# Self-attention in a decoder layer: the step's part of a projection is issued before the value matmuls, in the middle of the step

## The reference, cut to what matters

```python
qkv = x @ qkv_w + qkv_b
q, k, v = jnp.moveaxis(qkv.reshape(b, n, 3, H, D), 2, 0)
attn = jnp.einsum('bnhd,bmhd->bhnm', q, k) * scale
attn = jax.nn.softmax(attn, axis=-1)
out = jnp.einsum('bhnm,bmhd->bnhd', attn, v).reshape(b, n, c)
out = out @ proj_w + proj_b
```

## Time and profile before

| | |
|---|---|
| median of three runs | 4296.68 us |
| the profiled execution, its own time | 4303.63 us |
| its span, first to last instruction | 4302.0 us |
| TensorE busy over the span | 3724.0 us (87%) |
| granted TensorE clock, mean over the span | 0.932 |
| loop of self-attention | 202 to 2338 us of the span |

### The profile page before, as it was taken

One profiled execution on the slowest core, in us unless ns is written; L12 is line 12 of the kernel. 1 busy time (PEld: TensorE's weight loads), 2 busy tenths in 40 slices (PEclk: granted clock), 3 DMA queues, 4 the chain that ended last, 5 costly groups with the idle time before them and its releaser, 6 DMA issues. The chain is left out here.

```text
span 4302.0 us, 65605 instructions
## 1 busy us (share of the span) xinstructions
PE 3724.0 (87%) x17994; PEld 2267.9 (53%) x17995; DVE 2588.7 (60%) x4369; ACT 1651.5 (38%) x2902; POOL 2121.8 (49%) x1051
## 2 busy tenths in 40 slices
PE   4899999999999999999997688888549799887970
PEld 2445444454454544445454345445348688777860
DVE  3677776777767777677776454555324554444556
ACT  0055555555555555555554111111113343333430
POOL 0088888888888888888887112112220000000004
PEclk9799999999999999999998898898769899999985
DMA  5231211312113122131222201001022323233235
GB/s 190 82 88 44 80 54 50 93 39 80 56 48 94 38 80 58 47 94 38 80 57 70 75 30 59 29 29 59 10 78 95 120 79 108 89 106 101 98 101 171
DMA packets 202124, 322.52 MB, mean 75 GB/s; under 512 B 26107, under 2 KB 75675, under 8 KB 201797
## 3 DMA queue, kind: packets, MB, share of 16 engines
q1 hardware_dynamic: 182181, 266.45, 19.8%
q0 software_dynamic: 11168, 35.20, 2.6%
q10 hardware_dynamic: 8448, 16.78, 1.0%
HBM read 216.31 MB, written 46.44 MB: 61 GB/s over the span
## 5 line engine op out<-in xcount | busy, mean ns | idle before, releaser
L464 DVE TENSOR_REDUCE sa_part_max<-sa_mx 128x1 f32<-128x512 f32 x2124 | 1353.1, 681 | 575.7 <-PE sa_mx L579 573.5
L428 ACT ACTIVATE sa_prob<-sa_sc 128x512 f32<-128x512 f32 x2048 | 1117.9, 595 | 908.7 <-PE sa_sc L670 855.6
L268 POOL TENSOR_TENSOR sa_quad_sum<-sa_quad_sum,sa_prob 128x1024 f32<-128x1024 f32 x512 | 1205.3, 2393 | 0.0
L579 PE MATMUL sa_mx<-sa_k_stack,sa_q_stack 96*128 96x512 f32 x2124 | 1033.1, 491 | 23.2 <-issue 11.8
L670 PE MATMUL sa_sc<-sa_q_stack,sa_k_stack 98*128 98x512 f32 x2048 | 827.3, 404 | 7.4 <-ACT sa_prob L428 1.4
L268 POOL TENSOR_TENSOR sa_quad_sum<-sa_prob 128x1024 f32<-128x1024 f32 x256 | 617.3, 2433 | 406.0 <-ACT sa_prob L428 405.2
L579 PEld LDWEIGHTS sa_mx<-sa_k_stack,sa_q_stack 96*128 96x128 f32 x2124 | 407.6, 192 | 603.3 <-DVE sa_part_max L464 413.2
L1512 PE MATMUL ex_h<-ex_xT,ex_w 128*128 128x384 f32 (+2 forms) x2688 | 476.8, 334 | 117.0 <-issue 68.0
L593 PE MATMUL sa_pv<-sa_prob,sa_v 128*32 128x512 f32 x4104 | 552.1, 610 | 0.8 <-ACT sa_prob L428 0.8
L1512 PEld LDWEIGHTS ex_h<-ex_xT,ex_w 128*128 128x128 f32 x2688 | 457.8, 199 | 144.0 <-issue 121.7
L670 PEld LDWEIGHTS sa_sc<-sa_q_stack,sa_k_stack 98*128 98x128 f32 x2048 | 391.0, 191 | 176.1 <-ACT sa_prob L428 76.3
(11 more groups left out here) (178 smaller groups left out, 3397.9 us busy)
## 6 DMA issues: line engine op xcount, KB each, us to landing
sa_xT<-xT SPq DMA_DIRECT2D x70, 1024.0 KB, 5.2
ex_w_in<-in_L_ffn_w_dram SPq DMA_DIRECT2D x130, 512.0 KB
sa_k_stack<-sa_hilo SPq DMA_DIRECT2D x432, 64.0 KB, 2.0
sa_q_stack<-sa_hilo SPq DMA_DIRECT2D x408, 64.0 KB, 2.0
eo<-ex_out POOLq DMA_DIRECT2D x8, 1536.0 KB, 7.6
ca_aT<-attnT SPq DMA_DIRECT2D x9, 1024.0 KB, 7.1
ca_xb<-in_x_dram SPq DMA_DIRECT2D x9, 1024.0 KB, 9.0
attnT<-sa_recip SPq DMA_DIRECT2D x33, 256.0 KB, 2.4
```

The lines of the kernel that those rows point to most:

```text
L268: pool.tensor_tensor(quad_sum[:, i % 2, heads, :], so_far, prob[:, k, heads, :], ALU.add).then_inc(quad_ready, 1)
L428: act.activation(prob[:, kt % 4, j, :], sc[n % 2][:, :], ACT.Exp, scale=SCALE).then_inc(prob_ready, 1)
L464: dve.reduce_max(part_max[:, q, j, k:k + 1], mxp[bank % 3][:, :], AX_X).then_inc(max_read, 1)
L579: pe.matmul(mxp[bank % 3][:, :], q_stack[0:QK, j, at:at + P], k_stack[0:QK, buf, j, k * BANK:(k + 1) * BANK], start=True, stop=True).then_ ...
```

## The change

In each step that has a part of a projection, the call moves from behind head 3 to behind the score of head 1, ahead of `burst`. The instructions, their waits and their count stay the same; on the other engines nothing is edited.

```diff
                                 score(c, kt, i)
                                 if i == 1:
+                                    if (c, kt) in PART_AT:
+                                        project_part(*PART_AT[c, kt])
                                     burst(c, kt)
                                 if i == 2 and kt == T - EARLY:
                                     transpose_shift(at(NQ) + c + 1)
-                            if (c, kt) in PART_AT:
-                                project_part(*PART_AT[c, kt])
```

## The result

| | before | after |
|---|---|---|
| median | 4295.64 us (4 runs) | 4688.37 us (4678.99 to 4692.64, 4 runs) |
| span of the profiled execution | 4302.0 us | 4690.3 us |
| ratio to before | | 1.0911, 95% interval 1.0892 to 1.0931 |

The change makes the kernel 393 us, 9.1%, slower. The forecast was 4654 us, in a range of 4565 to 4745.

A forecast was written before the change was run, and what follows sets the result against it. The prediction took TensorE, in its written order, to bound the loop. Waits for `misc` (148 us), waits for exponentials (131) and clock falls (78) sum to 357 us, giving 4654 us, range 4565 to 4745.

The forecast's parts named there:

- term A: At kt 4 and kt 8, 64 first parts hold TensorE waiting for VectorE to release `misc`; 148 us.
- term B: At the end of all 384 steps with a part, scores wait for ScalarE's exponentials, 0.34 us each; 131 us.
- term C: Behind 60 of the 64 `misc` waits TensorE's granted clock falls to half, 1.3 us each; 78 us.
- The edits priced at nothing: Input DMAs, sequencing pauses at kt 0 and the 0.09 us passage from part to value matmuls: no added cost.
- (1): Rival: TensorE's clock holds through the single 2 to 3 us waits; 4576 us, chance 0.15.
- (2): Rival: the clock stays low longer, as in the 6.83 us stretch, another 78 us; 4732 us, chance 0.12.
- (3): Rival: exponentials don't bind at the step's end, as the longer middle lets ScalarE get ahead; 4523 us, chance 0.05.
- (4): Rival: `misc` is free in time, so no waits for it and no clock falls; 4428 us, chance 0.03.
- (5): Rival: faster, value weights load while the part streams, 35 us gained; 4262 us, chance 0.02.

The follow-up runs named there:

- e3: Changed kernel with 8 or 11 extra matmuls filling each of the 64 waits for `misc`; 4565.6 us, ratio 1.0632.
- e4: Changed kernel with VectorE taking the finished projection out of `misc` one step earlier; 4421.5 us, ratio 1.0295.
- e1: Changed kernel with the 64 first parts at kt 4 and kt 8 back at the step's end, 320 parts staying in the middle; 4415.0 us, ratio 1.0279.
- e5: Exponentials over 128 of 512 columns, attention not the reference's: on e4 4287.7 us (ratio 0.9988), on the kernel before 4268.8 us (0.9942).
- e2: Changed kernel with only the 64 first parts at kt 4 and kt 8 in the middle, the other 320 at the end; 4501.2 us, ratio 1.0481.
- e6: Kernel before, with VectorE emptying `misc` behind head 0's reading instead of head 1's and the four reciprocals one place earlier; 4264.1 us, ratio 0.9935.
- e10: e2 with its 64 waits filled by 8 matmuls (5 at kt 4 of chunk 3); 4438.1 us, ratio 1.0329.
- e8: e6 with the row sums of kt 14 moved from behind the value matmuls to the step's end; 4265.2 us, ratio 0.9932.

## Why the prediction was right, point by point

**The waits for `misc`, term A, 148 us: right, in place and length.** From the starts of scores in e3, at full clock, against before, less the 0.36 of term B, step by step: kt 4 of three chunks 7.55 - 4.57 - 0.36 = 2.62 us, kt 8 6.78 - 4.40 - 0.36 = 2.02, kt 4 of chunk 3 6.53 - 3.92 - 0.36 = 2.25. By 24, 32 and 8 this is 146 us. The 0.51 us that VectorE was to be later at kt 4 came out to the hundredth: 3.41 us behind the score, 2.90 before. e4 shows that the release, and not the matmuls behind it, is the cause.

**The exponentials, term B, 131 us: right.** 0.36 a step, 138 us over 384, of which 0.24 and 0.10 are the two waits of the earlier trace rows and the rest a few hundredths in the middle. e1 has it nearly alone (110 us for 320 steps), e5 removes it by its cause. So by the steps A and B make 284 us, where the sum had 279; at the starts of units 7 us go back, and the loops of e3 and of the kernel before differ by 279, the medians by 272. That the sum over the loop came out so exactly is in part luck, since I had priced nothing at the starts of units.

**The clock, term C, 78 us: the right count, too low a price.** The trace has a fall behind 60 of the 64 waits, as taken, but they cost 123 us by e3, 2.0 each and not 1.3. Two things were mis-sized. I had let only some last 6.83 us; 24 of the 60 do. And I had taken term B's 0.34 off the 1.49 us of the earlier trace rows, which wasn't due: a fall of 3.41 us costs 1.48, and most steps that have one still end with the 0.71 us of the wait for exponentials. Step by step, 36 x 1.48 + 24 x 2.45 = 112 us; the loops of the changed kernel and e3 differ by 116.5, with 4.5 at the starts of units. By the medians, C is 45 above its 78 and A with B 7 below their 279, so that the loss is 36 to 38 us above the 357 of the forecast. That these three add up to the measured loss proves nothing by itself, since C is what the changed kernel has over e3; the prices of single falls and waits are what bears it.

**The edits priced at nothing: right.** The DMAs keep up; first parts at kt 0 start 0.25 us behind the score, so no sequencing shows. From the start of a part to the value matmuls are 0.95 us, the part's two matmuls of 0.43 and the 0.09 of before. The Trainium skill ("TensorE: Matmul & The Clock Gate", Part 1, on queue depths) says that TensorE's queue can pull weight loads ahead of matmuls in flight. The trace does not show it for this passage: the first value weights are loaded at 1233.42, with the first value matmul, as after a score.

**The rivals.** (1), that the clock holds, is what e3 makes: 4566 us, where I had 4576. (2), 4732 us, took all falls for long ones; 24 of 60 were, and the result lies between it and the forecast. (3) fell with e5, (4) and (5) with the profile.

Left open is why the falls are fewer and shorter in e2: behind 42 of the 64 waits, 4 of them of 6.83 us, against 60 and 24 in the changed kernel. Length alone doesn't decide it: the eight waits of 2.1 us at kt 4 of chunk 3 are all followed by a fall in the changed kernel, and the 32 of 2.4 to 2.5 us at kt 8 by 28 there and by 24 in e2. In the changed kernel the waits for exponentials stand ahead of and behind each wait for `misc`, and at kt 4 the wait for `misc` is half a microsecond longer; no run parts the two.

## What to carry to other kernels

Work on the bounding engine that looks like mere load may stand where it does because it covers someone else's latency. Before moving it, list for both places what would be awaited there without it: here the end of a step needed it (exponentials, 0.34 us each of 384 times) and in the middle its own release was 2 to 3 us away. The cheaper repair for a wait is often in the order of the engine that releases it: moving VectorE's readout by one head, and the reciprocals out of its way, gave 28 us (e6), and moving the readout one step earlier in the changed kernel gave back 267 (e4). A new pause of TensorE costs itself and then the clock behind it: price both.

## What the runs showed of the hardware

- Filling 64 waits of 2.1 to 3.2 us with matmuls whose result is overwritten made the kernel 123 us faster. A fall of TensorE's granted clock to 0.50 behind such a wait cost 1.48 us where it lasted 3.41 us and 2.45 us where it lasted 6.83; a wait without a fall cost the same filled or not. None of the eight waits of 1.6 us at kt 4 of chunk 3 in e2 was followed by a fall: the step takes 5.87 us there, and 5.87 in e10, where it is filled.
- Row sums with 32-column weights cost 0.86 us behind value matmuls, and some 0.34 more (1.20 us, e8) when they stand alone between scores of full width; value matmuls cost 1.18 there.
